# An attention and shift kernel on one core: the residual goes out by its own transfer and the result is added to it in memory, key tile 7 of three head pairs is summed on VectorE, and one small statistics step changes places

## The reference, cut to what matters

```python
x = x + attention(groupnorm(x))      # 12 heads of 64 channels, N = 1024 tokens
x = x + displace(groupnorm(x))       # a shift per channel group, then a 3x3 blur

# attention: the scores are an outer product of two variances
var_v, var_k = var(v, axis=-1), var(k, axis=-1)
attn = softmax(var_v @ var_k.T * scale)
out = (attn @ v) @ W_proj.T + b_proj
```

## Time and profile before

| | us |
|---|---|
| median of 3 runs | 2106.61 (2103.96 to 2109.3) |
| the profiled execution | 2102.82 |
| its span in the trace | 2101.1 |
| TensorE busy | 2021.3 (96%) |
| VectorE busy | 1676.2 (80%) |
| ScalarE busy | 1176.4 (56%) |
| GpSimd busy | 233.7 (11%) |
| DMA moved | 214.34 MB, mean 102 GB/s |

### The profile page before, as it was taken

How to read it: one execution, slowest core, us unless ns; L and a number is a source line. 1 busy time by engine, 2 the same in 40 slices (tenths; PEclk the granted TensorE clock), 3 DMA queues, 4 the chain that set the end, 5 groups by cost and what they waited for, 6 DMA issues and landing times.

```text
span 2101.1 us, 33792 instructions
## 1 busy us (share of the span) xinstructions
PE 2021.3 (96%) x13060; PEld 1115.0 (53%) x13060; DVE 1676.2 (80%) x3593; ACT 1176.4 (56%) x1281; POOL 233.7 (11%) x280
## 2 busy tenths in 40 slices
PE   3799999999999999999999999999999999999997
PEld 2655447553466536654366633755356553665443
DVE  7487666998679876898759977699867987689857
ACT  5366733676257652767436673377625765376720
POOL 2000000110011100111001100011001110011111
PEclk8899999999999999999999999999999999999998
DMA  6411301345024340335213450143502434123314
GB/s 224 176 52 42 111 11 52 123 131 162 11 86 137 111 142 13 111 122 159 74 42 122 132 161 21 52 132 126 167 1 92 132 122 131 32 93 130 129 35 180
DMA packets 101313, 214.34 MB, mean 102 GB/s; under 512 B 48416, under 2 KB 49184, under 8 KB 101152
## 3 DMA queue, kind: packets, MB, share of 16 engines
q1 hardware_dynamic: 69184, 95.77, 15.1%
q0 software_dynamic: 25920, 94.38, 12.4%
q10 hardware_dynamic: 6048, 22.02, 3.4%
HBM read 154.07 MB, written 57.72 MB: 101 GB/s over the span
## 4 chain that ended last, share of the span: by engine, by line
PE 76%; DVE 9%; DMA 8%; ACT 3%; issue 2%; SPq 1%; POOL 1%; ACTq 0%; DVEq 0%
PE ps L1242 31%; PE ps L1277 24%; PE ps L1294 15%; PE ps L1259 4%; DMA a_sb<-a_rows 2%; ACT ring L645 2%; DVE bst_x L773 2%; DMA cs_rows_y<-mv_y 1%; DVE st L799 1%; DMA dt_sb<-d_sb 1%; DMA bt<-r_rows 1%; DVE d_sb L857 1%; DMA r_rows<-dt_sb 1%; DMA xv<-in_L_conv_W_qkv 1%; DMA gin_y<-cs_rows_y 1%
## 5 line engine op out<-in xcount | busy, mean ns | idle before, releaser
L645 ACT ACTIVATE ring<-a_sb,coef 128x1024 f32<-128x1024 f32 x768 | 813.9, 1137 | 21.4 <-PE ps L1277 10.8
L1242 PE MATMUL ps<-wkv_hi,h_sp 128*128 128x256 f16 x4608 | 778.0, 274 | 16.2 <-DVE h_sp L790 9.6
L1277 PE MATMUL ps<-ring,xv 128*64 128x512 f32 x3072 | 688.1, 597 | 0.5 <-ACT ring L645 0.3
L1242 PE MATMUL ps<-wkv_lo,h_sp 128*128 128x256 f16 x2304 | 631.2, 274 | 0.0
L1242 PEld LDWEIGHTS ps<-wkv_hi,h_sp 128*128 128x128 f16 x4608 | 452.5, 98 | 103.5 <-issue 30.6
L847 DVE TENSOR_TENSOR bt<-bt,ring 128x1024 f32<-128x1024 f32 x416 | 485.5, 1214 | 2.6 <-ACT ring L645 1.8
L1277 PEld LDWEIGHTS ps<-ring,xv 128*64 128x64 f32 x3072 | 209.0, 137 | 416.5 <-issue 398.5
L629 ACT ACTIVATE xv<-ps 128x256 f32<-128x256 f32 x192 | 72.5, 382 | 577.2 <-DVE st L799 577.1
L1294 PE MATMUL ps<-xv,wp_hi 128*128 128x512 f16 x1152 | 352.9, 383 | 0.0
L799 DVE BATCH_NORM_STATS2 st<-ps 128x6 f32<-128x64 f32 x1536 | 218.6, 214 | 121.0 <-PE ps L1242 120.2
L1242 PEld LDWEIGHTS ps<-wkv_lo,h_sp 128*128 128x128 f16 x2304 | 226.2, 98 | 27.1
(11 more groups left out here) (148 smaller groups left out, 1347.2 us busy)
## 6 DMA issues: line engine op xcount, KB each, us to landing
a_sb<-a_rows SPq DMA_DIRECT2D x96, 512.0 KB, 4.8
xv<-in_x POOLq DMA_DIRECT2D x48, 512.0 KB, 3.7
h_sp<-in_x ACTq DMA_DIRECT2D x42, 512.0 KB, 4.8
shift_rows<-bt POOLq DMA_DIRECT2D x42, 512.0 KB, 3.0
out<-xv POOLq DMA_DIRECT2D x42, 512.0 KB, 2.9
bt<-r_rows SPq DMA_DIRECT2D x80, 256.0 KB, 3.9
shift_rows<-ring SPq DMA_DIRECT2D x12, 528.0 KB, 14.8
xv<-in_L_conv_W_qkv SPq DMA_DIRECT2D x4, 1152.0 KB, 9.1
```

The costliest lines, as they stand in the source:

```text
L645: nc.scalar.activation(ring_of(p, s, m), a_sb[:, h % 4, :], ACT.Exp, scale=coef[:, h, m:m + 1]).then_inc(s_exp, 1)
L1242: last = nc.tensor.matmul(ps[:, kv_bank[u % 2], half * 2 * P:(half + 1) * 2 * P], h_sp[:, k, hp, m * P:(m + 1) * P], wkv[wpart][:, k, q * ...
L1277: last = nc.tensor.matmul(ps[s * HD:(s + 1) * HD, o_bank[p % 2] + j, :], v_sb[:, p, m, s * HD:(s + 1) * HD], ring_of(p, s, m)[:, j * HALF: ...
```

## The change

Four things are changed.

1. `MD` becomes (7, 8, 8, 8, 5, 5): key tile 7 of p = 1, 2, 3 goes into `acc` on VectorE. Its two additions stand after the pair's last `kv_stats` and ahead of `taps_x`. TensorE's `denominators` for that tile is gone, and its sum over `acc` is the only one of those pairs.
2. The first of the three x taps, which multiplied and added onto `x1`, becomes a ScalarE activation that overwrites `x1` with the product alone (`middle_tap_x`). It stands behind the exponentials of m = 5 and waits for the y taps, for `gn` of the next tile and for a new transfer.
3. That new transfer, on GpSimd's queue, writes `x1` of tile t to the output before it is overwritten, right behind `k_reduce` and ahead of the write of `g_t`. The old write of the tile, after the taps, now adds to what stands in DRAM.
4. In `phase_a`, `group_var` of y moves from behind unit 0 to behind unit 1, and `group_spread_y` from behind unit 1 to behind unit 2.

The last image is finished as before: its taps don't use the new transfer.

```diff
-        MD = (7, 7, 7, 7, 5, 5)
+        MD = (7, 8, 8, 8, 5, 5)
...
                         k_reduce(b + 1, t)
+                        pool.wait_ge(s_x1, (b + 1) * PU)
+                        hold(pool, s_held_pool)
+                        pool.dma_start(out_t[b, :, t, :], x1[:, t, :]).then_inc(s_res, 16)
                         pool.wait_ge(s_gn, b * CT + t + 1)
...
                         pool.wait_ge(s_fin, b * CT + t)
+                        pool.wait_ge(s_res, (b * CT + t) * 16)
                         hold(pool, s_held_pool)
-                        pool.dma_start(out_t[b, :, t - 1, :], x1[:, t - 1, :]).then_inc(s_out[t - 1], 16)
+                        pool.dma_start(out_t[b, :, t - 1, :], x1[:, t - 1, :], accum_op=ALU.add).then_inc(s_out[t - 1], 16)
...
+            def middle_tap_x(b, t):
+
+                act.wait_ge(s_pch, b * 3 * CT + 3 * t + 2)
+                act.wait_ge(s_gn, b * CT + t + 1)
+                act.wait_ge(s_res, (b * CT + t + 1) * 16)
+                nc.scalar.activation(x1[:, t, :], t_t, ACT.Copy, scale=taps[:, t, 0, 1:2]).then_inc(s_tapx, 1)
...
+                        if m == 5 and later:
+                            middle_tap_x(l1, p)
...
-                dve.wait_ge(s_pch, n + 2)
-                nc.vector.scalar_tensor_tensor(xt, tp, kx[:, 1:2], xt, ALU.mult, ALU.add).then_inc(s_pch, 1)
-                dve.wait_ge(s_pch, n + 3)
+                dve.wait_ge(s_tapx, b * CT + t + 1)
                 nc.vector.scalar_tensor_tensor(xt[:, :, 1:W], tp[:, :, 0:W - 1], kx[:, 0:1], xt[:, :, 1:W],
...
-                        if u == 0:
+                        if u == 1:
                             group_var(dve, "y", l1)
-                        if u == 1:
+                        if u == 2:
                             group_spread_y(dve, l1)
...
-                        add_up(b, p, m, later)
+                        if m < MT - 1:
+                            add_up(b, p, m, later)
...
+                            add_up(b, p, MT - 1, later)
                             if later:
                                 taps_x(l1, p, t_t)
...
                     pe.wait_ge(s_acc, b * NADD + ADDS_TO[p + 1])
-                    denominators([acc_of(p, s) for s in (0, 1)], False, True).then_inc(s_d, 1)
+                    if MD[p] == MT:
+                        d_bank_free(b, p, later)
+                    denominators([acc_of(p, s) for s in (0, 1)], MD[p] == MT, True).then_inc(s_d, 1)
```

More of the change, by code:

```diff
@@ L272, in gn_attention_displace @@
         s_pch = sem("s_pch")
+        s_tapx = sem("s_tapx")
+        s_res = sem("s_res")
         s_fin = sem("s_fin")
@@ L925, in taps_y_last @@
                                                ALU.mult, ALU.add).then_inc(s_pch, 1)
-                dve.wait_ge(s_pch, b * 4 * CT + 2 * i + 1)
+                dve.wait_ge(s_pch, b * 3 * CT + 2 * i + 1)
                 nc.vector.scalar_tensor_tensor(tp[:, 0:H - 1, :], sh[:, 1:H, :], ky[:, 2:3], tp[:, 0:H - 1, :],
@@ L953, in gn @@
                 elif wait_taps:
-                    dve.wait_ge(s_pch, b * 4 * CT + 4 * (t - 1) + 2)
+                    dve.wait_ge(s_pch, b * 3 * CT + 3 * (t - 1) + 2)
                 nc.vector.scalar_tensor_tensor(dst.rearrange("p (y x) -> p y x", x=W),
@@ L964, in taps_y @@
                 ky = taps[:, t, 1, :]
-                n = b * 4 * CT + 4 * t
+                n = b * 3 * CT + 3 * t
                 dve.wait_ge(s_tap, b * CT + t + 1)
@@ L977, in taps_x @@
                 kx = taps[:, t, 0, :]
-                n = b * 4 * CT + 4 * t
-                dve.wait_ge(s_pch, n + 2)
-                nc.vector.scalar_tensor_tensor(xt, tp, kx[:, 1:2], xt, ALU.mult, ALU.add).then_inc(s_pch, 1)
-                dve.wait_ge(s_pch, n + 3)
+                n = b * 3 * CT + 3 * t
+                dve.wait_ge(s_tapx, b * CT + t + 1)
                 nc.vector.scalar_tensor_tensor(xt[:, :, 1:W], tp[:, :, 0:W - 1], kx[:, 0:1], xt[:, :, 1:W],
                                                ALU.mult, ALU.add).then_inc(s_pch, 1)
-                dve.wait_ge(s_pch, n + 4)
+                dve.wait_ge(s_pch, n + 3)
                 nc.vector.scalar_tensor_tensor(xt[:, :, 0:W - 1], tp[:, :, 1:W], kx[:, 2:3], xt[:, :, 0:W - 1],
@@ L1092, in group_end @@
                     y_half_spread(1)
-                    dve.wait_ge(s_pch, b * 4 * CT + 2)
+                    dve.wait_ge(s_pch, b * 3 * CT + 2)
                     taps_mid_last(b, 0, tail_t[0])
@@ L1210, in last @@
                         taps_y_last(b, i)
-                        dve.wait_ge(s_pch, b * 4 * CT + 2 * i + 2)
+                        dve.wait_ge(s_pch, b * 3 * CT + 2 * i + 2)
                         mid = tail_t[i]
@@ L1261, in denominators, with d_bank_free @@
                 return last
+            def d_bank_free(b, p, later):
+                if p:
+                    pe.wait_ge(s_dsb, b * NR + p)
+                elif later:
+                    pe.wait_ge(s_rlast, b)
             def weigh(b, p, m, later):
@@ L1282, in weigh @@
                 if m >= MD[p]:
[L1283 to L1286, removed]
+                    if m == MD[p]:
+                        d_bank_free(b, p, later)
                     last = denominators([ring_of(p, s, m) for s in (0, 1)], m == MD[p], False)
```

## The result

| us | before | after |
|---|---|---|
| median (4 runs each) | 2105.28 (2102.41 to 2109.3) | 2070.56 (2067.16 to 2072.51) |
| profiled execution | 2102.82 | 2072.51 |
| its span | 2101.1 | 2070.8 |

The two traces lie 30.3 us apart.

What follows compares the result with a forecast made beforehand. TensorE was taken as the bound, VectorE close behind. The terms -21.4 - 5.2 + 8.6 = -18.0 us took 2106.6 to a forecast of 2088.6 us, with a range from 2073 to 2103.

Steps and rivals of the forecast that it cites:

- The crossing: From p = 4 to p = 5: later exponentials 1.2, residual write 1.3, tap gone -1.27, in seven images, 8.6 us lost.
- One sum less on TensorE: In three pairs of eight images, 24 calls of 0.89 us go and count in full: 21.4 us gained.
- Two additions more on VectorE: In p = 1 to 3, 2.43 us a pair, hidden before TensorE's last sum with 3 us to spare.
- The statistics step: At unit 1's statistics, `group_var` no longer waits for its transfer; 5.2 us of TensorE's eviction wait go.
- Nothing is lost from p = 4 to 5: Rival: transfers fit in and the wait for the reciprocal goes, -35.4 us, 2071; chance 0.13.
- Gives it all back: Rival: p = 4 to 5 pays the full 4.2 us of transfers, 2109, or half, 2100; chance 0.11.
- VectorE becomes the bound: Rival: in p = 1 to 3 VectorE waits for transfers 1 to 2 us more a pair, 2094 to 2115; chance 0.09.
- Slow adding write: Rival: an adding write beyond 18 us delays the reload and the bias; at 20 us, 2145; chance 0.07.
- 192 matmuls: Sign in the trace after: 24 x 8 = 192 fewer sum matmuls on the ring.
- the exponentials of p = 5 a good us later: Sign in the trace after: ScalarE's first exponentials of p = 5 a good us later relative to TensorE.
- a landing below 18 us: Sign in the trace after: the adding write lands in less than 18 us; some 6 us was taken.
- No wait of TensorE's sums for VectorE's additions: Sign in the trace after: TensorE's sums never wait for VectorE's additions; such waits in p = 1 to 3 refute the prediction.

Runs made afterwards that it cites:

- sums_only: Kernel before with only key tile 7 of p = 1 to 3 moved to VectorE, x taps untouched; ratio to before 0.9989.
- no_residual: Kernel after without the residual's own write and without the adding, so seven images lack the residual; 2060.77 us, ratio to before 0.9782.
- tap_only: Kernel before with only the x tap on ScalarE, the residual's own write and the adding write; ratio to before 0.9931.
- late_group_eight: Kernel after with last reciprocal early, x `group_var` behind two evictions, key tile 7 of p = 0 also on VectorE; 2082.51 us, ratio to before 0.9881.
- twice_recip: Kernel after with VectorE taking the last reciprocal twice, one behind the other; 2113.01 us, ratio to before 1.0035.

## Why the prediction was wrong

Two steps failed; had only one of them failed, the result would lie inside the range. The crossing was charged with 8.6 us and cost 1.7, because the step added two delays that run side by side. And TensorE's clock was put at nothing, without a reason; it gave back 5.1 us between the two traces and, by an estimate below, some 10 in the runs. Point by point, by the prediction's own steps:

- *One sum less on TensorE, -21.4.* The mechanism was right, the size a little high. A call is worth 0.86 and not 0.89, and some 1.2 us of short waits are left: -19.4.
- *Two additions more on VectorE, met "with 3 us to spare".* Right in the result, wrong in the place. L1274 waits 0.8 us in all, but the deadline that binds is the transpose in p = 4, which the step didn't name. sums_only missed it by 2.4 us an image. With the shorter taps it is kept; VectorE's lag was weighed against the wrong event.
- *The statistics step, -5.2.* Right; 6.3 by the spacing of the matmuls. The idle column undercounts, as the modelled ends of the matmuls run into the gap.
- *The crossing, 7 x (1.2 + 1.3 - 1.27) = +8.6.* Measured +1.7, so this term was mis-sized by 6.9. The 1.2 stood for ScalarE's later exponentials and the 1.3 for the residual's write. Both end at the same event, the first two exponentials of p = 5, which need ScalarE free and the broadcast of `a` landed, and only the later of the two counts. The timelines of one crossing of the kernel after, ScalarE first, then the chain:

```profile
725.13 1.14 ACT L691 ACTIVATE xv<-bt,taps 128x1024 f32<-128x1024 f32 x1
...
730.33 1.04 ACT L677 ACTIVATE xv<-bt 128x1024 f16<-128x1024 f32 x1
...
733.48 2.31 ACT L651 ACTIVATE ring<-a_sb,coef 128x1024 f32<-128x1024 f32 x2 [1.06 <-issue]
```

```profile
722.16 6.50 DMA a_rows<-at
...
729.12 5.49 DMA a_sb<-a_rows
```

ScalarE is done with the split and the bias and still stands idle for 1.06 us. The two exponentials of m = 0 then start, the second at 734.6, just as the broadcast has landed (729.12 + 5.49). Counted from the last transpose, and as averages over six images, the exponentials of m = 7 came 1.5 us later than before and the split 0.6; the broadcast landed at 13.1 instead of 12.1, and the second exponential of p = 5 started at 13.1 instead of 12.1. The next events moved likewise: the copy of the sums from 17.3 to 18.4, `o_normalise` from 31.2 to 32.8, the last reciprocal from 42.0 to 42.3. Between the last two stands the tap that is gone, and 1.6 - 0.3 is about its 1.27. Without the transfers (no_residual) the broadcast lands at 12.3, the copy is at 17.5 and `o_normalise` at 31.0, with ScalarE's activation still in place: that activation alone delays what follows by 0.2 us at most. So the two charges were 1.6 together and not 2.5, and they go with the transfers. In tap_only, which has these edits alone, the crossing is even 2.1 us shorter than before; why it is 3.8 us longer beside the other two edits is not isolated. The step also counted seven crossings where six can lose anything: the last image's takes 43.7 us in both traces, which is TensorE's own work.

- *What the sum left out: TensorE's clock.* The waits for the reciprocal were counted at their length (8.8) and taken to stay, "the reciprocal that TensorE waits for". They fell to 4.9, and behind such a wait the clock could fall to 0.50 for some us: 6.8 us lost in the trace before, 1.7 in that after. The medians differ by 34.7 and the traces by 30.3. The granted clocks on record point to the same cause: the mean of 56 runs of before is 0.9856, that of the four of after 0.9905, and 0.0049 of 2100 us is 10 us, the 5.1 and about as much again as the missing 4.4. This is an estimate, as these means hold the startup too.

In the numbers: 8.6 - 1.7 = 6.9 from the crossing, 5.1 from the clock, 1.1 from the eviction, less 2.0 from the sums, and 1.2 of small things, are the 12.3 us between -18.0 and -30.3. The last 4.4, to the medians, are most likely more of the clock.

Of the rivals, "Nothing is lost from p = 4 to 5" gave 2071 and came out at the time measured, with a chance of 0.13, but by luck. It let the wait for the reciprocal vanish (-8.8) and the crossing cost nothing; 4.9 us of the wait were left and the crossing grew by 1.7. What made up for it was the clock, which the rival didn't have. "Gives it all back" fell: the adding write is free and the residual's write costs 1.3 to 1.6 us an image, not 4.2. Its working also has a slip: with half of the 4.2 us the sum gives 2094 and not 2100. "VectorE becomes the bound" is false for the whole change; in its neighbours sums_only and late_group_eight VectorE does bind, by its own additions and not by the waits that the rival named. "Slow adding write" fell at a median of 5.4 us and a longest of 9.3.

Of the views announced, these came out: 192 matmuls, a period of 31.06, 0.4 us of eviction wait left, the exponentials of p = 5 a good us later, a landing below 18 us. "No wait of TensorE's sums for VectorE's additions" came out but for 0.8 us in two places.

## What to carry to other kernels

A wait of the bounding TensorE has to be priced at its length plus what the clock may lose behind it: look at the granted clock in short stretches behind each wait before summing, since busy shares hide it. Delays that end at the same event are not added; ask which of them comes last. When work is moved onto a second bound, follow its lag to the next thing that the first engine needs from it, a pair further on if need be; the deadline isn't always the buffer that the work fills. And edits that look independent may pay for each other, as the tap for the sums, or remove the same loss, as here the clock's.

## What was unexpected of the hardware

- A wait of TensorE of 1 to 2 us is sometimes followed by some us at 0.50 and sometimes not, at the same place in the same program: three dips in one execution of before, five in the next (the same three images and two more). Behind 1.10 us in one image the clock fell, behind 1.47 us in another (after) it didn't, and tap_only's three waits of up to 2.0 us brought none. One dip in before cost 1.7 to 3.4 us. Behind seven waits of 2.4 us in sums_only it came three times, behind seven of 2.5 us in late_group_eight five times, and in twice_recip, with waits of 1.6 to 4.6 us, in every image.
- An adding transfer of 512 KB from SBUF to DRAM took 5.4 us from issue to landing in the median of 42, against 2.9 for a plain one, and its issue on GpSimd 0.93 us against 0.56. In a crowded stretch the two were alike: the reload waited 7.8 us for the adding one and 8.2 for the plain one of before.
- A large write costs where small transfers of a chain lie beside it, though nothing waits for it there. After, the 8 KB of `a_rows` landed in 6.50 us at the crossing shown above, against 4.82 before and 1.4 in the median of all places.
